# Token statistics of six of sixteen batches on ScalarE, and new step lists for the opening

## The chip, the cores and the metric

The kernel runs on one core of a Trainium2 chip. The metric is the device time of one execution in microseconds (us). The kernel before takes 1945.47 us, the median of three runs (1943.98 to 1945.88).

## What is computed

The input `x` is 16 batches of 512 tokens of 256 numbers, f32. Each token is normalised, and the result goes two ways: through an attention layer with a feed-forward block, and through a gated network whose operands are rounded to a 4-bit grid in blocks of 16. Cut to what matters here:

```
xn = (x - mean(x)) / sqrt(var(x) + 1e-5)          # per token; also needed summed over the tokens of a batch
pooled = xn.mean(axis=1)                           # one row of 256 per batch, all 16 batches
gl  = pooled @ gate_w + gate_b + einsum(pooled @ mod_w + mod_b, mod_basis)
wts = topk_sparse(gl)                              # 16 heads x 16 modes per batch
kern_masks = einsum(amps, sin(freqs . position + phases))
kern = einsum(wts, kern_masks)                     # 16 heads x 512 lags per batch
scores = 3 * step(kern) * window + q bias + k bias + 0.15 * qc . kc / sqrt(8)
s = LN(h + ffn(h)),  h = LN(xn + softmax(scores) @ v @ out_w + out_b)
g = silu(fp4_linear(silu(fp4_linear(xn, w_gate)) * fp4_linear(xn, w_up), w_down))
out = x + s * g
```

The kernel masks need `pooled` of all sixteen batches, so before any batch's scores can be finished, the statistics (mean and variance of each token) of all of `x` must have been taken.

## The kernel before

Tokens lie on the 128 partitions, four tiles `t` to a batch (`[128, 4, 256]`). The program has three parts: a head (steps named `pre:`, `pro:` and `first:`), a loop over batches 1 to 14 (`mid`), and an end. On each of the five engines the steps of a part stand in an order written out by hand in the table `ORDER`; an engine does its steps strictly in that order, and waits at a step's semaphores with everything behind it. The change touches the head's five lists, and the steps `st` and `cp`; the loop and the end are as they were.

In the head, `pre:` is the work that is common to all batches, `pro:` the first half of batch 0, `first:` the rest of batch 0 together with the start of batch 1.

- `px.n` (SyncE) loads batch n into one of NX = 4 buffers (`hY`, `y2`, shown as `y` in the trace, `xnb`, `catT`). From n = 4 on it waits until TensorE's sum of batch n - 4 has let go of the buffer.
- `st.n` (VectorE) takes the statistics: four BN_STATS, a small copy, four BN_AGGR, and the addition of eps into `p_ve`. `rs.n` (GpSimd) raises that to the power -1/2. `cp.n` (VectorE) files mean and 1/std with three small copies, the last into `v_cur`, from which TensorE reads its weights.
- `sum.n+1` (TensorE) adds batch n, weighted by 1/std, to the sums in PSUM (8 passes); `sum.0` clears the sums, `sum.17` takes the means off. `pre:pooled` (VectorE) reads them.
- `arg.h`, `rnd.h`, `fr.h`, `sin.h` for 16 heads: TensorE makes the arguments, ScalarE rounds them, VectorE takes the fraction, ScalarE the sine. `arg.h` waits for `fr.h-4`, since there are four PSUM banks.
- `pre:ones` (GpSimd) is three large memsets, of `KS`, `QS` and `v_new`.
- `pro:norm`, `xT`, `proj.0` to `.2`, `projm`, `splitio`, `load.0`, `load.1`: batch 0 is normalised, transposed, projected, split into bf16 parts, and goes to DRAM and back. `pro:v.0` and `.1` make the values, `mx.h.p.u` are the tiles of the row maxima (TensorE computes 20 of them for half 0, VectorE reduces each).
- `ws.i` (VectorE), `wm.i` (GpSimd), `wr.i` (VectorE), `wt` (TensorE, ScalarE): the three matrices of the gated network are rounded and transposed.
- After `pre:pooled`: `modT`, `peak`, `topk`, `kw`, `soft` (VectorE) with `mod`, `gl`, `wide`, `kern` (TensorE) and the first loads `first:T` of the kernel's rows.

Of the kernel before, what the change touches and what calls it, by code (L numbers as in the profile page):

```python
# [56 lines left out]
class Event:  # L57
# [5 lines left out]
    def wait(self, eng, b, k=None):  # L63

        if isinstance(b, int) and b < 0:
# [10 lines left out]
            pre:px.0 pre:waves pre:px.1 pre:px.2 pre:ld.w_proj pre:px.3 pro:xload pre:px.4 pre:px.5 pre:px.6 pre:px.7  # L76
            pre:ld.w_gate pre:ld.w_v pre:ld.basis pre:ld.c0 pre:px.8 pre:ld.c1 pre:ones pre:px.9 pro:splitio pre:px.10
            pre:px.11 pro:load.0 pre:px.12 pre:px.13 pre:px.14 pre:px.15 pro:load.1 pre:ld.c2 pre:ld.w_rest pre:rz
            first:xload pro:mio.0 pre:rows first:T.0 first:T.1 first:splitio first:T.2 first:T.3 first:mio.1 first:T.4
            first:load.0 first:T.5 first:T.6 first:T.7 first:mio.0  # L80
        """,
        gpsimd="""
            pre:iota pre:half pre:rs.0 pre:rs.1 pre:rs.2 pre:rs.3 pre:rs.4 pre:rs.5 pre:rs.6 pre:ones pro:projm.0
            pre:rs.7 pro:projm.1 pro:projm.2 pre:wm.0.0 pre:rs.8 pre:rs.9 pre:rs.10 pre:rs.11 pre:wm.0.1 pre:wm.1.0
            pre:rs.12 pre:rs.13 pre:rs.14 pre:rs.15 pre:wm.1.1 pro:xq first:xnb pre:wm.2.0 pre:wm.2.1 pro:xr first:xq
            first:projm.0 first:xr first:projm.1 first:projm.2 first:mul.0 first:mul.1 first:mul.2 first:hq.0
            first:mul.3 first:hr.0 first:hq.1 first:mul.4 first:hq.2 first:mul.5 first:hr.1 first:hr.2 first:mul.6
            first:mul.7 first:hq.3 first:hr.3
        """,
        vector="""  # L90
            pre:zero pre:st.0 pre:cp.0 pre:st.1 pre:cp.1 pre:st.2 pre:fr.0 pre:fr.1 pre:cp.2 pre:st.3 pre:fr.2
            pre:cp.3 pre:fr.3 pro:norm pre:st.4 pre:fr.4 pre:st.5 pre:fr.5 pre:st.6 pre:cp.4 pre:st.7 pro:proj.0
            pre:fr.6 pre:fr.7 pre:fr.8 pre:cp.5 pre:cp.6 pre:fr.9 pro:xq pro:proj.1 pre:fr.10 pro:proj.2 pre:ws.0
            pre:fr.11 pre:st.8 pre:fr.12 pre:fr.13 pre:cp.7 pre:wr.0 pre:st.9 pre:ws.1 pre:cp.8 pre:cp.9 pro:v.0
            pro:v.1 pre:st.10 pre:st.11 pre:fr.14 pre:cp.10 pro:mx.0.0.0 pro:mx.0.0.1 pro:mx.0.0.2 pro:mx.0.0.3
            pro:mx.0.0.4 pro:mx.0.1.0 pro:mx.0.1.1 pro:mx.0.1.2 pro:mx.0.1.3 pro:mx.0.1.4 pro:mx.0.2.0 pro:mx.0.2.1
            pro:mx.0.2.2 pro:mx.0.2.3 pro:mx.0.2.4 pro:mx.0.3.0 pro:mx.0.3.1 pre:cp.11 pre:st.12 pre:st.13 pre:st.14
            pre:cp.12 pre:st.15 pre:cp.13 pro:mx.0.3.2 pro:mx.0.3.3 pro:mx.0.3.4 pre:cp.14 pre:cp.15 pro:mfin.0 pre:mr
            pre:wr.1 pre:pooled pre:fr.15 pre:poolT first:mx.1.0.0 pre:modT pre:peak first:mx.1.0.1 pre:topk pro:xr
            pre:kw pre:ws.2 first:mx.1.0.2 first:mx.1.0.3 first:norm pro:xr2 pre:wr.2 first:mx.1.0.4 first:mx.1.1.0  # L100
            first:mx.1.1.1 first:mx.1.1.2 pre:soft first:proj.0 first:xq first:proj.1 first:xr first:v.0 first:proj.2
            first:xr2 first:mx.1.1.3 first:mx.1.1.4 first:muld.0.0 first:mx.1.2.0 first:mx.1.2.1 first:mx.1.2.2
            first:muld.0.1 first:mx.1.2.3 first:muld.1.0 first:muld.1.1 first:mx.1.2.4 first:mx.1.3.0 first:mx.1.3.1
            first:mx.1.3.2 first:mx.1.3.3 first:mx.1.3.4 first:mfin.1 first:muld.2.0 first:silu.0.0 first:muld.2.1
            first:silu.0.1 first:muld.3.0 pre:pad first:hq.0 first:muld.3.1 first:v.1 first:hr.0 first:silu.1.0
            first:silu.1.1 first:muld.4.0 first:hq.1 first:muld.4.1 first:silu.2.0 first:mx.0.0.0 first:silu.2.1
            first:muld.5.0 first:mx.0.0.1 first:mx.0.0.2 first:hq.2 first:mx.0.0.3 first:muld.5.1 first:hr.1
            first:mx.0.0.4 first:mx.0.1.0 first:dn.0 first:ctxt.0 first:muld.6.0 first:silu.3.0 first:mx.0.1.1
            first:mx.0.1.2 first:silu.3.1 first:hr.2 first:muld.6.1 first:mx.0.1.3 first:mx.0.1.4 first:mx.0.2.0
            first:muld.7.0 first:mx.0.2.1 first:ctxt.1 first:muld.7.1 first:mx.0.2.2 first:mx.0.2.3 first:mx.0.2.4  # L110
# [1579 lines left out]
```

## Time and the profile before

| | us |
|---|---|
| median of 3 runs | 1945.47 |
| the profiled execution | 1947.52 |
| its span, first to last instruction | 1945.7 |
| first tile of the row maxima on VectorE | from 75.93 |
| `pre:pooled` on VectorE | from 115.56 |
| `pre:soft` on VectorE | from 153.79 |
| end of the head (`cT`, the first step of the loop on TensorE) | from 252.64 |

The profiled execution lies 1.8 us over its span, and 2.05 us over the median. In the rows below a time is us from the span's start. PE is TensorE, PEld its weight loads, DVE VectorE, ACT ScalarE, POOL GpSimd, SP SyncE.

### The profile page before, as it was taken

The page shows a single profiled execution, that of the slowest core. Times are in us where ns is not written, and L with a number is a line of the kernel's source. Part 1 is how long each engine was busy: PE and PEld are TensorE (multiplying, and loading weights), DVE is VectorE, ACT ScalarE, POOL GpSimd, SP SyncE. Part 2 cuts the span into 40 slices and gives each one's busy share as a digit, 9 for nine tenths or more (in the row PEclk, how much of TensorE's full clock was granted, in tenths as well). Part 3 has the DMA queues.
Part 4 walks back from the last instruction along what each step waited for, and adds up shares of the span by engine and source line. Part 5 has one row for each costly group of instructions (what it writes and reads, how often), then busy time and mean ns, then how long its engine had stood idle before and what let it go on. Part 6 is the DMA issues. An engine that isn't in the chain of part 4 may idle for free.

```text
span 1945.7 us, 42571 instructions
## 1 busy us (share of the span) xinstructions
PE 1820.7 (94%) x12700; PEld 1311.4 (67%) x12700; DVE 1615.3 (83%) x5197; ACT 901.9 (46%) x1833; POOL 1103.7 (57%) x799
## 2 busy tenths in 40 slices
PE   8667999999999999999999999999999999999997
PEld 3234677676776767677776767677676767677766
DVE  7868879888898988888997988888897988889763
ACT  3024454454635445453545445463545445363542
POOL 3434746565664746465674756466574656566563
PEclk8777999999999999999999999999999999999999
DMA  5343223232223333232322323222332323322211
GB/s 170 117 123 89 64 74 108 65 105 73 77 74 83 108 73 95 65 103 70 93 76 73 107 75 95 73 82 71 99 90 73 107 62 103 77 78 74 63 56 33
DMA packets 138566, 165.35 MB, mean 85 GB/s; under 512 B 19758, under 2 KB 100655, under 8 KB 138453
## 3 DMA queue, kind: packets, MB, share of 16 engines
q1 hardware_dynamic: 138458, 164.30, 30.5%
q14 instruction: 87, 0.70, 0.1%
q8 instruction: 21, 0.34, 0.1%
HBM read 127.85 MB, written 36.41 MB: 84 GB/s over the span
## 4 chain that ended last, share of the span: by engine, by line
PE 60%; DVE 15%; issue 12%; POOL 6%; ACT 3%; DMA 3%; SPq 1%; DVEq 0%; ACTq 0%; POOLq 0%
PE ps L767 11%; PE ps L758 11%; PE ps L699 8%; PE ps L716 4%; PE ps L622 3%; PE ps L609 3%; PE ps L656 3%; PE ps L595 3%; POOL Pr L1174 3%; PE ps L672 2%; PE ps L731 2%; PE ps L652 2%; DVE st L956 2%; DVE nmax L1035 2%; DMA QS<-q_bias_parts 2%
## 5 line engine op out<-in xcount | busy, mean ns | idle before, releaser
L1174 POOL TENSOR_TENSOR Pr<-Pr,Tz 128x768 f32<-128x768 f32 (+2 forms) x384 | 478.2, 1275 | 248.5 <-ACT Pr L831 244.6
L1035 DVE CUSTOM_DVE_ANT_0 ps<-ps,future 128x512 f32<-128x512 f32 (+3 forms) x1024 | 474.6, 516 | 51.2 <-issue 50.9
L831 ACT ACTIVATE Pr<-ps 128x384 f32<-128x384 f32 x512 | 243.8, 489 | 352.7 <-PE ps L656 348.6
L622 PE MATMUL ps<-KS,QS 108*128 108x512 bf16 (+3 forms) x1024 | 218.3, 304 | 32.5 <-DVE nmax L1035 23.9
L758 PE MATMUL ps<-catT,w 128*128 128x256 f32 x1024 | 237.8, 380 | 0.7 <-ACT catT L894 0.7
L767 PE MATMUL ps<-w,gT 128*128 128x256 f32 x1024 | 232.9, 381 | 0.9 <-ACT gT L911 0.9
L1065 DVE SCALAR_TENSOR_TENSOR Pr<-ps,Tz 128x512 f32<-128x512 f32 x256 | 175.2, 684 | 54.7 <-ACT ps L820 46.7
L820 ACT ACTIVATE ps<-ps 128x512 f32<-128x512 f32 x256 | 150.4, 588 | 139.9 <-PE ps L652 138.4
L767 PEld LDWEIGHTS ps<-w,gT 128*128 128x128 f32 x1024 | 190.8, 190 | 25.7 <-ACT gT L911 1.3
L758 PEld LDWEIGHTS ps<-catT,w 128*128 128x128 f32 x1024 | 189.6, 190 | 26.3 <-ACT catT L894 0.9
L716 PE MATMUL ps<-wdT,hqT 128*128 128x256 f32 x768 | 178.0, 381 | 0.7 <-ACT hqT L870 0.7
L656 PE MATMUL ps<-QS,KS 112*128 112x384 bf16 (+2 forms) x768 | 162.7, 276 | 16.1 <-DVE Pr L1065 11.7
L699 PE MATMUL ps<-wgT,xqT 128*128 128x352 f32 x512 | 176.0, 466 | 0.2 <-ACT xqT L851 0.2
L699 PE MATMUL ps<-wuT,xqT 128*128 128x352 f32 x512 | 172.4, 459 | 0.0
L1213 POOL TENSOR_TENSOR slot<-slot 128x704 f32<-128x704 f32 x64 | 107.6, 1681 | 97.5 <-DVE slot L939 97.5
L622 PEld LDWEIGHTS ps<-KS,QS 108*128 108x128 bf16 x1024 | 88.2, 98 | 106.7 <-DVE nmax L1035 48.5
L1223 POOL TENSOR_TENSOR rstd<-ve,minus_half 128x4 f32<-128x4 f32 (+1 forms) x34 | 33.4, 982 | 223.4 <-DVE ve L964 222.0
L716 PEld LDWEIGHTS ps<-wdT,hqT 128*128 128x128 f32 x768 | 142.4, 190 | 20.1 <-ACT hqT L870 1.1
L672 PE MATMUL ps<-Pr,v_cur 128*17 128x128 f32 (+2 forms) x3584 | 152.5, 321 | 0.6 <-ACT hqT L870 0.6
L1035 DVE DVE_READ_ACCUMULATOR2_ANT nmax<- 128x1 f32 x1024 | 142.7, 139 | 0.0
L699 PEld LDWEIGHTS ps<-wuT,xqT 128*128 128x128 f32 x512 | 97.2, 190 | 54.4 <-ACT ctxT L846 0.3
L672 PEld LDWEIGHTS ps<-Pr,v_cur 128*17 128x17 f32 x3584 | 95.2, 98 | 53.2 <-issue 40.8
(226 smaller groups left out, 3252.0 us busy)
## 6 DMA issues: line engine op xcount, KB each, us to landing
Tz<-kernel_rows SPq DMA_DIRECT2D x256, 256.0 KB, 3.5
KS<-k_parts SPq DMA_DIRECT2D x32, 384.0 KB
QS<-q_parts SPq DMA_DIRECT2D x64, 192.0 KB
hY<-in_x SPq DMA_DIRECT2D x19, 512.0 KB, 4.8
xn<-in_x SPq DMA_DIRECT2D x17, 512.0 KB, 3.5
out<-y SPq DMA_DIRECT2D x15, 512.0 KB, 3.0
q_parts<-q_sp SPq DMA_DIRECT2D x16, 384.0 KB, 3.1
k_parts<-k_sp SPq DMA_DIRECT2D x16, 384.0 KB, 2.4
```

Source lines behind the costliest of these rows:

```text
L622: ins = mm(o, QS[0:KROWS, 2 * p + e, it * P:(it + 1) * P], KS[0:KROWS, p, 0:n], start=True, stop=True)
L656: ins = mm(dst[:, at:at + PAST[j]], KS[0:SROWS, p, j * P:(j + 1) * P], rhs[:, S - 1:P * (j + 1) - 1:-1], start=True, stop=True)
L672: ins = mm(dst[32 * hh:32 * hh + HD + 1, to:to + n], v_cur[:, j, 4 * g + hh, :], rhs[:, n - 1::-1], start=i == 0, stop=i == len(pieces) - 1)
L699: ins = mm(dst[:, 0:IH], xqT[:, c, t * P:(t + 1) * P], wt[:, c, f * IH:(f + 1) * IH], start=c == 0, stop=c == KD - 1)
L716: ins = mm(dst[:, 0:D], hqT[:, c * P:(c + 1) * P], wdT[:, c, :], start=c == 0, stop=c == KI - 1)
L758: ins = mm(dst[:, i * n:(i + 1) * n], w1[:, c, f * P:(f + 1) * P], catT[:, c, hf * n:(hf + 1) * n], start=c == 0, stop=c == KD - 1)
L767: ins = mm(dst[:, 0:D], gT[:, f, at:at + P], w2[:, f, :], start=f == 0, stop=f == KF - 1)
L820: inc(af(src, src, ACT.Exp), "a_exp")
L831: inc(af(Pr[:, p % 4, e, at:at + wd], src[:, 0:wd], ACT.Exp), "a_exp")
L1035: ins = v.tensor_tensor_reduce(o, o, future[:, S - n:S], -1.0, 3e38, ALU.add, ALU.min, nmax[:, 2 * pl + e, it:it + 1])
L1065: v.scalar_tensor_tensor(blocks(Pr[:, p % 4, e, 0:S]), blocks(ps[:, SC_BANKS[n % len(SC_BANKS)], :]), 3e38, near, ALU.min, ALU.mult).then_ ...
L1174: ins = g.tensor_tensor(a, a, Tz[:, p % 2, :, P * j:P * j + PAST[j]], ALU.mult)
```

## The change

The statistics of batches 5, 7, 9, 11, 13 and 15 are taken by ScalarE, in two passes over the data: a Copy of each of the four tiles with an accumulated output gives the sum, one small Copy turns the four sums into minus the mean, and a Square of each tile with that as bias and an accumulated output gives the sum of squared differences. VectorE's `st.n` of these batches is then one small instruction (divide by 256, add eps) that waits for ScalarE (`rowsq`), and the first of the copies in `cp.n` becomes a division by 256. A new buffer `junk` takes the outputs that nobody reads. The counts of the semaphore `stats` follow the ten batches that are left.

```diff
+        ACT_STATS = [5, 7, 9, 11, 13, 15]
+        junk = sb("junk", [P, T, D])
...
+                if n in ACT_STATS:
+                    dve.wait_ge(L["rowsq"], ACT_STATS.index(n) + 1)
+                    v.tensor_scalar(p_ve[:, i, :], p_st[:, i, :, 2], 1.0 / D, EPS, ALU.mult, ALU.add).then_inc(L["var"], 1)
+                    return
+                k2 = 2 * sum(m not in ACT_STATS for m in range(n))
                 for t in range(T):
                     ins = v.bn_stats(p_st[:, i, t, :], x_in[i][:, t, :])
                 ins.then_inc(L["stats"], 1)
-                dve.wait_ge(L["stats"], 2 * n + 1)
+                dve.wait_ge(L["stats"], k2 + 1)
...
+                if n in ACT_STATS:
+                    v.tensor_scalar(mean_all[:, T * n:T * (n + 1)], p_st[:, i, :, 0], 1.0 / D, None, ALU.mult)
+                else:
+                    v.tensor_copy(mean_all[:, T * n:T * (n + 1)], p_mv[:, i, :, 0])
...
+            elif k == "st":
+                n = s[1]
+                i, m = n % NX, ACT_STATS.index(n)
+                act.wait_ge(x_sem[i], 16 * (n // NX + 1))
+                if n >= NX:
+                    act.wait_ge(L["mean"], n - NX + 1)
+                if m:
+                    act.wait_ge(L["rowsq"], m)
+                for t in range(T):
+                    ins = af(junk[:, t, :], x_in[i][:, t, :], ACT.Copy, accum_out=p_st[:, i, t, 0:1])
+                ins.then_inc(L["rowsum"], 1)
+                act.wait_ge(L["rowsum"], 2 * m + 1)
+                af(p_st[:, i, :, 1], p_st[:, i, :, 0], ACT.Copy, scale=-1.0 / D).then_inc(L["rowsum"], 1)
+                act.wait_ge(L["rowsum"], 2 * m + 2)
+                for t in range(T):
+                    ins = af(junk[:, t, :], x_in[i][:, t, :], ACT.Square, bias=p_st[:, i, t, 1:2], accum_out=p_st[:, i, t, 2:3])
+                ins.then_inc(L["rowsq"], 1)
```

All five lists of the head are laid out anew. The diff of them is a table of names; what it does is shown here at three places, as the instructions then stand in an engine's stream. In SyncE's list `px.2` to `px.7` stand behind more of the weight loads, and the first load of batch 1 behind `mio.0`; on TensorE eleven `arg` steps and the transposes of batch 0 now come ahead of the first sum, and `sum.9` ahead of `pro:v.0`; the remaining rows of the lists are permutations of the same steps.

First, GpSimd at its first statistics step. Before (KS, QS and v_new are the memsets of `pre:ones`, p_rstd is `rs.n`):

```order
L1357 MEMSET minus_half 128x4
L1373 TENSOR_TENSOR p_rstd<-p_ve,minus_half 128x4 x7
L1353 MEMSET KS 128x4096
L1354 MEMSET QS 128x4096
L1355 MEMSET v_new 128x1088
L1166 TENSOR_TENSOR q_sp<-q_r,q_sp 128x512
```

And with the change:

```order
L1358 MEMSET minus_half 128x4
L1374 TENSOR_TENSOR p_rstd<-p_ve,minus_half 128x4
L1354 MEMSET KS 128x4096
L1355 MEMSET QS 128x4096
L1356 MEMSET v_new 128x1088
L1374 TENSOR_TENSOR p_rstd<-p_ve,minus_half 128x4 x4
```

The three memsets stood behind the seventh `rs`, and stand now behind the first.

Second, VectorE from its first statistics on. Before (L1414 to L1422 are `st`, L1429 to L1431 `cp`, all of batch 0 and then batch 1):

```order
L1414 BN_STATS p_st<-hY 128x6 x4
L1417 COPY p_ve<-p_st 128x4
L1419 BN_AGGR p_mv<-p_st 128x2 x4
L1422 TENSOR_SCALAR p_ve<-p_mv 128x4
L1429 COPY mean_all<-p_mv 128x4
L1430 COPY rstd_all<-p_rstd 128x4
L1431 COPY v_cur<-p_rstd 128x4
L1414 BN_STATS p_st<-y 128x6 x4
```

With the change (L1444 is `fr`, L992 `pro:norm`, L1420 the next `st`):

```order
L1444 SCALAR_TENSOR_TENSOR Pr<-Pr,ps 128x512
L1438 COPY mean_all<-p_mv 128x4
L1439 COPY rstd_all<-p_rstd 128x4
L1440 COPY v_cur<-p_rstd 128x4
L1444 SCALAR_TENSOR_TENSOR Pr<-Pr,ps 128x512 x6
L992 TENSOR_SCALAR xn<-xn,mean_all,rstd_all 128x256 x4
L1420 BN_STATS p_st<-y 128x6 x4
```

One `fr` comes ahead of the copies of batch 0, six more and the normalisation of batch 0 come directly behind them, and the statistics of batch 1 after all of that.

Third, ScalarE at its first new step, and VectorE where that is waited for. ScalarE with the change (L1613 is `rnd`, L1617 `sin`, L1627 to L1633 the statistics, first of batch 5 and then of batch 7):

```order
L1613 ACTIVATE Pr<-ps,round_c 128x512 x2
L1627 ACTIVATE junk,p_st<-y 128x256 x4
L1630 ACTIVATE p_st<-p_st 128x4
L1633 ACTIVATE junk,p_st<-y,p_st 128x256 x4
L1613 ACTIVATE Pr<-ps,round_c 128x512
L1617 ACTIVATE Pr<-Pr 128x512
L1627 ACTIVATE junk,p_st<-catT 128x256 x4
```

VectorE there (L1460 is the last instruction of `ws.0`, L1416 the short `st.5`, then `st.6`, and L1436 of the short `cp.5`):

```order
L1460 TENSOR_SCALAR gs_old<-gs_old 128x96
L1416 TENSOR_SCALAR p_ve<-p_st 128x4
L1420 BN_STATS p_st<-xnb 128x6 x4
L1423 COPY p_ve<-p_st 128x4
L1425 BN_AGGR p_mv<-p_st 128x2 x4
L1428 TENSOR_SCALAR p_ve<-p_mv 128x4
L1436 TENSOR_SCALAR mean_all<-p_st 128x4
```

No table load of ScalarE stands between these steps and the sines around them. VectorE's short step stands at the place of a whole `st`, and everything behind it waits with it for ScalarE.

## Rows read from the trace of the kernel before

**Rows 1.** The page: span, and each engine's busy time.

```profile
span 1945.7 us, 42571 instructions
PE 1820.7 (94%) x12700; PEld 1311.4 (67%) x12700; DVE 1615.3 (83%) x5197; ACT 901.9 (46%) x1833; POOL 1103.7 (57%) x799
```

**Rows 2.** Windows: PE, PEld, DVE, ACT, POOL busy (xinstructions), then clock, DMA share, GB/s.

```profile
0.00:115.56 115.56, 84.46 (x255) 32.77 (x255) 91.01 (x357) 24.33 (x40) 43.19 (x40) 0.79 0.57 167
75.93:115.56 39.63, 29.71 (x108) 10.24 (x108) 28.35 (x151) 4.20 (x7) 16.28 (x11) 0.82 0.60 174
115.56:153.79 38.23, 19.59 (x95) 11.48 (x95) 29.13 (x85) 7.49 (x9) 13.52 (x7) 0.70 0.06 18
176.56:252.64 76.08, 68.15 (x538) 44.20 (x539) 61.88 (x207) 34.07 (x74) 49.91 (x39) 0.89 0.26 79
```

**Rows 3.** The timeline at the head's checkpoints, and one row of three `fr`.

```profile
7.93 0.69 ACT L1604 ACTIVATE Pr<-ps,round_c 128x512 f32<-128x512 f32 x1 [2.82 <-PE ps L1543]
...
8.07 0.17 DVE L1429 COPY mean_all<-p_mv 128x4 f32<-128x4 f32 x1 [1.28 <-POOL p_rstd L1373]
...
39.49 1.87 DVE L1435 SCALAR_TENSOR_TENSOR Pr<-Pr,ps 128x512 f32<-128x512 f32 x3
...
49.13 0.35 DVE L1008 SCALAR_TENSOR_TENSOR bias_r<-ps,bb,bias_sp 128x128 f32<-128x128 f32 x1 [2.23 <-ACT bias_sp L798]
...
75.93 0.69 DVE L1035 CUSTOM_DVE_ANT_0 ps<-ps,future 128x512 f32<-128x512 f32 x1
...
115.56 0.41 DVE L1463 TENSOR_SCALAR ctxn<-ps 16x256 f32<-16x256 f32 x1 [2.86 <-PE ps L1535]
...
153.79 1.73 DVE L1504 TENSOR_SCALAR Tz<-Pr 128x2048 f32<-128x2048 f32 x1
```

**Rows 4.** The timeline around 31 us, GpSimd and VectorE.

```profile
30.82 3.51 POOL L1353 MEMSET KS<- 128x4096 bf16 x1
31.34 7.41 DVE L1417 COPY p_ve<-p_st 128x4 f32<-128x4 f32 x1
...
34.27 3.51 POOL L1354 MEMSET QS<- 128x4096 f32 x1
...
37.72 1.00 POOL L1355 MEMSET v_new<- 128x1088 f32 x1
```

**Rows 5.** The timeline, one batch's statistics on VectorE.

```profile
27.70 1.40 DVE L1414 BATCH_NORM_STATS2 p_st<-xnb 128x6 f32<-128x256 f32 x4
...
29.61 0.17 DVE L1422 TENSOR_SCALAR p_ve<-p_mv 128x4 f32<-128x4 f32 x1
29.69 0.16 DVE L1429 COPY mean_all<-p_mv 128x4 f32<-128x4 f32 x1
```

**Rows 6.** The timeline, ScalarE: eight instructions in a row with a bias, eight without.

```profile
278.30 3.16 ACT L911 ACTIVATE gT<-ps,b 128x256 f32<-128x256 f32 x8
...
153.91 1.58 ACT L1622 ACTIVATE wgT<-ps 128x128 f32<-128x128 f32 x8 [9.21 <-PE ps L1589]
```

**Rows 7.** The page's groups: an accumulator read on VectorE.

```profile
L1035 DVE DVE_READ_ACCUMULATOR2_ANT nmax<- 128x1 f32 x1024 | 142.7, 139 | 0.0
```

**Rows 8.** The timeline, TensorE: a sum at either clock, and a projection at the low one.

```profile
17.75 3.59 PE L1530 MATMUL ps<-y,v_cur 128*16 128x256 f32 x8
...
45.16 1.90 PE L1530 MATMUL ps<-y,v_cur 128*16 128x256 f32 x8
...
30.64 3.78 PE L595 MATMUL ps<-xnT,cq 128*128 128x512 f32 x4
```

**Rows 9.** Two stretches of 2 us: busy times, then clock.

```profile
18.00:20.00 2.00, 2.00 (x6) 0.74 (x5) 1.65 (x7) 0.55 (x1) 0.32 (x1) 0.50 0.00 0
46.00:48.00 2.00, 2.00 (x8) 0.81 (x7) 0.91 (x2) 0.17 (x1) 0.00 (x0) 1.00 1.07 353
```

**Rows 10.** The chain that ended last, 90 to 116 us: start, length, what.

```profile
96.29 6.80 DMA catT<-in_x
...
113.72 1.74 PE ps L1535 x8
```

More of the change, by code:

```diff
@@ L75 @@
         sync="""
[L76 to L80, printed above, removed]
+            pre:px.0 pre:waves pre:px.1 pre:ld.w_proj pro:xload pre:px.2 pre:px.3 pre:ld.w_gate pre:px.4 pre:ld.w_v
@@ L81 @@
+            pre:ld.basis pre:ld.c0 pre:px.5 pre:px.6 pre:ones pre:ld.c1 pre:px.7 pre:px.8 pre:px.9 pro:splitio
+            pre:px.10 pro:load.0 pre:px.11 pre:px.12 pre:px.13 pre:px.14 pre:px.15 pro:load.1 pre:ld.c2 pre:ld.w_rest
+            pro:mio.0 pre:rz first:xload pre:rows first:T.0 first:T.1 first:splitio first:T.2 first:T.3 first:mio.1
+            first:T.4 first:load.0 first:T.5 first:T.6 first:T.7 first:mio.0
         """,
         gpsimd="""
-            pre:iota pre:half pre:rs.0 pre:rs.1 pre:rs.2 pre:rs.3 pre:rs.4 pre:rs.5 pre:rs.6 pre:ones pro:projm.0
@@ L84 @@
[L84 to L88, printed above, removed]
+            pre:iota pre:half pre:rs.0 pre:ones pre:rs.1 pre:rs.2 pre:rs.3 pre:rs.4 pro:projm.0 pro:projm.1
@@ L89 @@
         """,
         vector="""
[L91 to L110, printed above, removed]
@@ new lines @@
+            pre:mr pro:mfin.0 pre:wr.1 pre:pooled pre:fr.15 pre:poolT first:mx.1.0.0 pre:modT pre:peak first:mx.1.0.1
+            first:mx.1.0.2 pre:topk pre:kw pre:ws.2 first:mx.1.0.3 pro:xr first:norm pro:xr2 pre:wr.2 first:mx.1.0.4
+            first:mx.1.1.0 first:mx.1.1.1 first:mx.1.1.2 pre:soft first:proj.0 first:xq first:proj.1 first:proj.2
+            first:mx.1.1.3 first:mx.1.1.4 first:mx.1.2.0 first:mx.1.2.1 first:xr first:xr2 first:muld.0.0 first:v.0
+            first:muld.0.1 first:mx.1.2.2 first:mx.1.2.3 first:muld.1.0 first:mx.1.2.4 first:mx.1.3.0 first:mx.1.3.1
@@ new lines @@
+            pre:sum.13 pre:sum.14 pro:mx.0.3.4 pre:sum.15 pre:sum.16 pre:sum.17 first:mx.1.0.0 pre:poolT pre:mod
+            pre:gl first:mx.1.0.1 first:mx.1.0.2 first:mx.1.0.3 pro:mT.0 pre:wt.0 pre:wide pre:kern pre:wt.1
+            first:mx.1.0.4 first:mx.1.1.0 first:mx.1.1.1 pre:wt.2 pre:wt.3 first:mx.1.1.2 first:xT.0 first:xT.1
+            first:proj.0 pre:wt.4 pre:wt.5 pre:wt.6 pre:wt.7 pre:wt.8 first:proj.1 first:proj.2 first:sc.0.0 pro:xqT
+            first:sc.0.1 first:mx.1.1.3 first:mx.1.1.4 first:mx.1.2.0 pre:join first:mx.1.2.1 first:gu.0.0
```

109 lines of the change are left out of this document (61 added, 48 removed).

## Prediction

> **What bounds the kernel now.** The page comes first: TensorE is busy 94% of the span and VectorE 83% [rows 1], but these are means over a long loop that the change doesn't touch. So I cut the head out by windows. Up to `pre:pooled` (115.56 us) VectorE is busy 91.0 us, TensorE 84.5 and ScalarE 24.3 [rows 2]; TensorE's clock is 0.79 of full speed there, so it isn't at its peak. From 115.56 to 153.79 VectorE has 29.1 of 38.2 us; in the last 76 us TensorE leads with 68.2 [rows 2]. The order is fixed on each engine, and everything behind `pooled` (gates, masks, `soft`, first scores) waits for it. So the question is how early `pooled` and then `soft` come [rows 3]; behind them the same work stands as before, and I carry a shift there one for one to the end.
>
> VectorE's 91.0 us aren't all work. At 31.34 a copy of `[128, 4]` takes 7.41 us instead of 0.17, and its row ends at 38.75, where GpSimd's three memsets end (30.82 to 38.72) [rows 4]. So 7.2 us of the busy time are a blocked copy; useful work is 83.8 us, and idle 115.6 - 91.0 = 24.6 us.
>
> **The change part by part.**
>
> *Work taken from VectorE.* One batch's statistics last from 27.70 to 29.69, where the next step's copy begins: 1.99 us [rows 5]. Six times is 11.9 us. Each leaves one small instruction (0.08 from start to start, 29.61 to 29.69 [rows 5]), 0.5 us in all. Useful work up to `pooled` falls by 11.4 us, from 83.8 to 72.4. No other VectorE step crosses `pooled`, by the two lists.
>
> *Work given to ScalarE.* The trace has no Copy or Square with an accumulated output. From below: eight instructions of 256 columns with a bias take 3.16 us, 0.395 each; 128 columns without one 0.20 each [rows 6]. A batch is 4 Squares at 0.395, 4 Copies at some 0.30 (between these two rows) and one small Copy at 0.2: 3.0 us, if accumulating is free. From above: a second instruction as long as the short one, 0.20, for each of the eight gives 4.6. VectorE's own accumulator read is 0.14 [rows 7], and being the same kind of operation it is what I take: 3.0 + 8 x 0.14 = 4.1, and with two waits on its own results 4.3 us a batch. Six are 26 us, on an engine that idles 91 of 115.6 us [rows 2]: hidden, except where VectorE's short step meets an unfinished ScalarE.
>
> *The blocked copy.* The memsets stand now behind `rs.0`, so they run from about 8.0 (in the rows `cp.0` starts at 8.07, as soon as `rs.0` is done [rows 3]) to 15.9, 7.9 us later. VectorE does one `fr` first: its rounding ends at 8.6 [rows 3] and it takes 0.6 (three in 1.87 [rows 3]), so the three copies of `cp.0` are due at 9.2 and get through at 15.9. The stall isn't removed but moved: 6.7 us in place of 7.2. The Trainium skill has a rule for this (SBUF — State Buffer, "Who interferes with whom"): VectorE and GpSimd share a port pair that one holds for a whole instruction, and copies in the two-port mode ask for it. The trace agrees with its 7.41 us. It speaks against the new place, since there too plain copies meet the memsets; without the rule one might expect no stall, and the sum below would be 6.7 us smaller.
>
> What is behind the copies: six `fr`, `norm`, and the whole statistics of batches 1 to 3; on TensorE `arg.5` on, since `arg.h` waits for `fr.h-4`.
>
> *The new front.* TensorE now has eleven `arg` before the first sum. Half speed is the level of 1.2 GHz: at clock 0.50 a sum takes 3.59 us, at 1.00 1.90; the four passes of a projection take 3.78 at the low one, so some 1.9 at the full [rows 8, 9]. An `arg` is two passes of that width, half of 3.78, and 1.7 in a row, where one begins before the last has ended. The engine stands idle before 16.8, so I take `arg.5` to `arg.10` low: 10.3 us, to 27.1. The transposes and `sum.0` take 2, `sum.1` 3.5 (low): 32.6. Then `proj.0`, `sum.2`, `proj.1`, `sum.3` at full clock, 1.9 each, and `proj.2` 0.8: 41. VectorE's last projection step, at 49.13 before [rows 3], comes about 41.2. But by then VectorE lacks work that it had done before (`fr.7` to `.10` at 0.6, `cp.3` to `.6` at 0.22, `st.6` at 2.0: 5.3 us). At equal work the change is ahead by 2.6 us only. In this stretch VectorE runs dry: it has done `xq` by 30.6 and has 3.2 us of work till 41.2, so 7.4 us idle.
>
> *New waits.* (1) `st.5` stands at the head of VectorE's queue behind `ws.0`; ScalarE begins it when batch 5 has landed, near 45, and ends near 49.3, some 1.5 us late. (2) `st.7` stands behind `rnd.13` on ScalarE, that waits for `arg.13`, that for `sum.7`, that for `cp.6`: some 2 us late. (3) `wr.0` waits for GpSimd's product and `ws.0` for its load: 3.5 together. Then `v.0` and `v.1` wait on TensorE for `sum.8` and `sum.9`: two sums and the values at mixed clock, 3.5 us of waiting. From the first maximum tile to `pooled` the rows have 39.6 us with 28.4 busy [rows 2]. The same steps stand there now, but `st.13` and `st.15` are short: 28.4 - 2 x 1.9 = 24.6 us of work. The idle 11.3 us came from sums of batches 8 to 10 between the tiles, from the load of batch 15 (6.8 us) and from the last sums, each 1.7 us [rows 10]. Now TensorE has two of these sums ahead of the values, and batch 15 can be loaded some 10 us behind the first tile instead of 20; I take 4.1 us of waits, an estimate of mine, for `sum.10` to `sum.12` between the tiles and for the last one. That makes 28.7 us.
>
> *The ledger up to `pooled`.* Useful 72.4, blocked 6.7, idle 4.0 (start, till 9.2) + 7.4 + 7.0 (waits 1 to 3) + 3.5 + 4.1 = 26.0. Sum 105.1 us, against 115.6: 10.5 earlier. The first maximum tile comes at 105.1 - 28.7 = 76.4, so no earlier than 75.93 [rows 3]; the gain shows behind it, because the sums are further on and their batches wait less.
>
> *Behind `pooled`.* The same VectorE steps. One more maximum tile stands before `topk` (0.8 later), and the 1.4 us of `pro:xr`, which filled VectorE's wait for `wide`, stands behind it now: I take 1 us lost in the 38.2. Table loads: by the lists there are two fewer of ScalarE, at a place where it waits anyway: nothing. From `soft` on, VectorE's order to the first score changes, but the load of the kernel's rows sets it: nothing, with 3 us either way for the 76 us of the new `first` list.
>
> Sum: 10.5 - 1.0 = 9.5 us. The profiled execution 1947.5 - 9.5 = 1938.0; the median lies 2.05 below that execution: 1936 us.
>
> **The rivals.**
>
> *The gain is larger: the waits don't come.* If TensorE is at full clock for the `arg` steps and sums (as for part of 12 to 15 us), the front is shorter by up to 6 x 0.85 = 5 us, and waits 1 to 3 shrink too. All 7 us of those two give 1929. For it: DMA and ScalarE have room. Against: clock 0.79 in the head [rows 2]. Chance 0.25.
>
> *The gain goes into the front.* `sum.1` comes at 32 instead of 9 us, so batch 4 is loaded 20 us later than now, and if every TensorE step from 27 on runs at the low clock, `proj.2` comes 6 us later (four steps at 3.6 instead of 1.9). Then 9.5 - 6 to 7 leaves about 3: 1943, and a little more makes it no change. For it: the low clock right after `arg` steps (0.50 at 18 to 20 us [rows 9]). Against: under a steady load the clock came back in that stretch each time. Chance 0.17.
>
> *Slower: ScalarE's statistics are what VectorE waits for.* VectorE meets them at its queue's head at `st.5`, `st.7`, `st.9` and, through `cp.15`, at `pooled`. Each us over 4.3 for a batch is paid up to four times; 9.5 / 4 = 2.4, so from 6.7 us a batch the gain is gone, and from 7.7 the kernel is 4 us slower, 1949.5. That would be 0.9 us for an instruction whose nearest row is 0.395 [rows 6]. Such a price could come from table loads, but the lists have none there. Chance 0.06.
>
> *The change does what it says to VectorE, but `first` gives it back.* The last 76 us are TensorE's (68.2 busy [rows 2]) and newly ordered; 5 us lost there leave 4.5: 1941. This lies in the main range. The forecast itself has 0.52.
>
> **How the numbers follow.** Main range: ScalarE's price from 3.0 to 4.6 moves two to four waits by up to 1.3 us down and 0.3 up, 3 up and 1 down in all; `first` gives 3 either way, the clock in the front 3: 1931 to 1941. To hold 8 in 10 I reach to 1929 below and 1943 above. 0.2% (3.9 us) is about what a measurement of this kernel can tell from no change: up to 1941.6 is faster. Faster: 0.52 + 0.25 + a quarter of the front case, 0.04 = 0.81. Same: the rest of that case, 0.12, and 0.01. Slower: the ScalarE case, 0.06.
>
> **What would show it.** Right: a copy of `cp.0` of 6 to 7 us beside the memsets at 8 to 16; no such row at 31; `bias_r` near 41; the first maximum tile near 76; `pooled` near 105 and `soft` near 144; the loop's first `cT` some 9 us before 252.6. ScalarE's statistics take 4 us a batch, with a row of its own for the accumulator. Wrong in a step: `pooled` on time but `cT` not earlier (`first`); waits of VectorE for ScalarE of 3 us and more at the short steps (its price); no blocked copy at 9 us. What would make the forecast wrong as a whole is most likely what is late between 41 and 76 us, where one wait replaces another and I have placed four of them by estimate.

## The result, and the profile after

The changed kernel takes 2046.03 us (median of 4 runs, 2044.12 to 2050.88) against 1945.68 of the kernel before on the same chip: ratio 1.0521, 95% interval 1.0500 to 1.0542. It is 5% slower, and the forecast was 1936.

The page of the kernel after, which answers to [rows 1], and one row of its DMA queues:

```profile
span 2045.5 us, 42628 instructions
PE 1860.2 (91%) x12700; PEld 1332.3 (65%) x12700; DVE 1641.4 (80%) x5143; ACT 925.3 (45%) x1933; POOL 1110.6 (54%) x799
...
q14 instruction: 99, 0.81, 0.1%
```

TensorE has 40 us more of busy time for the same 12,700 matmuls, and queue 14, which brings instructions, has 99 packets; in the kernel before it was 87. VectorE has 54 instructions fewer, and 26 us more of busy time.

First the opening, in windows as in [rows 2] (up to `pooled`, the first maximum tile to `pooled`, `pooled` to `soft`, the last 76 us ahead of the loop):

```profile
0.00:113.23 113.23, 82.74 (x251) 31.94 (x251) 80.15 (x302) 49.28 (x144) 40.45 (x38) 0.85 0.57 170
81.78:113.23 31.45, 24.61 (x96) 8.63 (x96) 24.46 (x132) 13.76 (x48) 7.81 (x6) 0.84 0.67 202
113.23:155.57 42.34, 24.32 (x113) 14.67 (x113) 29.28 (x85) 6.05 (x13) 17.76 (x9) 0.61 0.06 17
174.46:250.54 76.08, 68.80 (x555) 45.68 (x555) 65.64 (x203) 33.44 (x74) 51.18 (x38) 0.96 0.31 91
```

The timeline of VectorE at the checkpoints of [rows 3], with the copies that meet GpSimd's memsets (here 7.84 to 15.75, [rows 4] before) and the two short steps that wait for ScalarE:

```profile
9.43 6.34 DVE L1438 COPY mean_all<-p_mv 128x4 f32<-128x4 f32 x1
...
40.26 0.35 DVE L1007 SCALAR_TENSOR_TENSOR bias_r<-ps,bb,bias_sp 128x128 f32<-128x128 f32 x1 [1.40 <-ACT bias_sp L797]
...
49.85 0.17 DVE L1416 TENSOR_SCALAR p_ve<-p_st 128x4 f32<-128x4 f32 x1 [2.25 <-ACT junk L1633]
...
53.40 2.57 DVE L1438 COPY mean_all<-p_mv 128x4 f32<-128x4 f32 x1
...
65.37 1.54 DVE L1416 TENSOR_SCALAR p_ve<-p_st 128x4 f32<-128x4 f32 x1 [4.30 <-ACT junk L1633]
...
79.47 0.75 DVE L1018 TENSOR_TENSOR v_new<-ps,row_v_b 128x256 f32<-128x256 f32 x2 [3.57 <-PE ps L608]
...
81.78 0.69 DVE L1034 CUSTOM_DVE_ANT_0 ps<-ps,future 128x512 f32<-128x512 f32 x1
...
113.23 0.41 DVE L1472 TENSOR_SCALAR ctxn<-ps 16x256 f32<-16x256 f32 x1
...
155.57 3.25 DVE L1513 TENSOR_SCALAR Tz<-Pr 128x2048 f32<-128x2048 f32 x1
```

So the opening isn't where 100 us went: `pooled` comes 2.3 us earlier than before, `soft` 1.8 later, the loop's first `cT` at 250.54, 2.1 earlier. The loss is in the loop, whose steps the change doesn't touch. A window from the loop's first `cT` to its fifteenth (14 iterations), in before and in after, with two single iterations of after between them, the first and the fourth:

```profile
252.64:1801.13 1548.49, 1502.51 (x10865) 1111.71 (x10864) 1329.27 (x4270) 761.27 (x1540) 915.99 (x658) 1.00 0.31 84
```

```profile
250.54:361.10 110.56, 107.32 (x777) 79.33 (x776) 94.75 (x305) 54.36 (x110) 65.41 (x47) 1.00 0.31 85
598.00:717.49 119.49, 111.76 (x778) 82.05 (x777) 97.74 (x305) 54.62 (x110) 65.89 (x47) 0.96 0.28 78
250.54:1900.97 1650.43, 1543.32 (x10865) 1132.46 (x10864) 1363.79 (x4270) 764.45 (x1540) 922.15 (x658) 0.97 0.28 79
```

Same counts of instructions, 101.9 us more. And the first iteration is as fast as before (110.56 us); every later one takes 117 to 120. Whatever is wrong, then, isn't in what the loop's instructions do but in coming round to them again.

The same place in two iterations, from the timelines of VectorE, GpSimd and TensorE. Before (the iteration's `cT` is at 473.73):

```profile
477.70 0.69 DVE L1133 TENSOR_TENSOR hY<-ps,xnb 128x512 f32<-128x512 f32 x1 [2.94 <-PE ps L731]
479.43 0.69 DVE L1133 TENSOR_TENSOR hY<-ps,xnb 128x512 f32<-128x512 f32 x1 [1.03 <-PE ps L731]
...
487.63 1.67 DVE L978 SCALAR_TENSOR_TENSOR hY<-hY,rstd,row_ln_b 128x256 f32<-128x256 f32 x4
...
489.22 3.73 POOL L1174 TENSOR_TENSOR Pr<-Pr,Tz 128x768 f32<-128x768 f32 x3 [6.00 <-ACT Pr L831]
```

After (`cT` at 478.28):

```profile
482.34 0.69 DVE L1132 TENSOR_TENSOR hY<-ps,xnb 128x512 f32<-128x512 f32 x1 [3.02 <-PE ps L730]
486.97 0.69 DVE L1132 TENSOR_TENSOR hY<-ps,xnb 128x512 f32<-128x512 f32 x1 [3.94 <-issue]
...
495.17 4.22 DVE L977 SCALAR_TENSOR_TENSOR hY<-hY,rstd,row_ln_b 128x256 f32<-128x256 f32 x4
...
495.79 4.19 POOL L1173 TENSOR_TENSOR Pr<-Pr,Tz 128x768 f32<-128x768 f32 x3 [5.02 <-ACT Pr L830]
...
499.52 1.96 PE L747 MATMUL ps<-ident,hY 128*128 128x128 f32 x8 [3.54 <-DVE hY L977]
...
504.48 3.62 PE L757 MATMUL ps<-catT,w 128*128 128x256 f32 x8
```

Three things happen one after the other. (1) Between the two sums into `hY` VectorE stands for 3.94 us, and the reason is "issue": it waited for nothing that the profile shows. Before, it waited there 1.03 us for TensorE, so it is 2.9 us late. (2) Its group L977 starts 16.9 us behind `cT` instead of 13.9. Before, the group was over (489.30) just when GpSimd's products began (489.22); now the products begin 0.6 us into it, the two run into each other, and the group takes 4.22 us instead of 1.67, another 2.55. (3) TensorE waits 3.54 us for it, and behind the wait its clock is at the lower level, as three windows of the kernel after show:

```profile
496.00:499.50 3.50, 0.00 (x0) 0.00 (x0) 3.50 (x5) 0.58 (x1) 3.50 (x3) 0.84 0.00 0
499.50:504.00 4.50, 4.12 (x20) 3.12 (x21) 3.57 (x16) 2.76 (x6) 4.50 (x3) 0.50 0.38 117
504.00:508.20 4.20, 4.20 (x11) 2.98 (x10) 2.07 (x10) 0.63 (x2) 0.60 (x1) 0.50 0.37 125
```

0.50 is 1.2 GHz; eight matmuls of L757 take 3.62 us there, and 1.89 a little later. The iteration is 9.2 us longer than before; 2.9 and 2.55 are named, and the remaining 3.7 fit 8.7 us of TensorE at half speed, which is 4.35 us of work lost. Not every iteration loses as much. The 13 slow ones are 7.8 us longer in the mean, and they differ with the clock: the second takes 117.18 us at a granted clock of 0.99, the ninth 118.64 at 0.97, the fourth 119.49 at 0.96.

The packets of queue 14 bear this out, though the profile doesn't say which engine one of them is for. In the iteration above the kernel after has one that starts between 480.0 and 480.4 us (480.14), and the next between 484.6 and 485.0 (484.76, landed at 485.26):

```profile
q14 instruction: 1, 0.01, 7.1%
```

```profile
q14 instruction: 1, 0.01, 7.8%
```

The second sum starts at 486.97. In all 13 iterations from the second on the second packet starts 4.4 to 5.0 us behind the first, and the second sum 1.6 to 1.8 us behind the second packet's landing. In before the same two packets come behind each jump (475.60 and 479.99 in the iteration shown), and the second sum, at 479.43, doesn't wait for the second of them. In the first iteration there is no such pair in either kernel.

### The profile page after: what moved, and what is told of

It is laid out like the page before. It is cut to its first block, busy times and chain, and to the rows that moved or that the text cites. A ratio compares the mean times of both kernels' runs of the same rounds, so it can differ in the third digit from the quotient of the medians.

```text
span 2045.5 us, 42628 instructions
## 1 busy us (share of the span) xinstructions
PE 1860.2 (91%) x12700; PEld 1332.3 (65%) x12700; DVE 1641.4 (80%) x5143; ACT 925.3 (45%) x1933; POOL 1110.6 (54%) x799
## 4 chain that ended last, share of the span: by engine, by line
PE 59%; DVE 17%; issue 15%; POOL 5%; ACT 3%; DVEq 1%; ACTq 0%; DMA 0%; POOLq 0%; SPq 0%
PE ps L757 11%; PE ps L766 10%; PE ps L698 8%; PE ps L715 4%; PE ps L621 3%; PE ps L655 3%; PE ps L730 3%; POOL Pr L1173 3%; PE ps L608 3%; PE ps L594 3%; PE ps L651 2%; PE ps L671 2%; DVE hY L977 2%; DVE st L955 2%; DVE nmax L1034 1%
## 5 line engine op out<-in xcount | busy, mean ns | idle before, releaser
L1173 POOL TENSOR_TENSOR Pr<-Pr,Tz 128x768 f32<-128x768 f32 (+2 forms) x384 | 485.0, 1292 | 297.6 <-ACT Pr L830 294.3
L621 PE MATMUL ps<-KS,QS 108*128 108x512 bf16 (+3 forms) x1024 | 227.2, 315 | 29.9 <-DVE nmax L1034 27.5
L757 PE MATMUL ps<-catT,w 128*128 128x256 f32 x1024 | 248.2, 392 | 0.7 <-ACT catT L893 0.7
L757 PEld LDWEIGHTS ps<-catT,w 128*128 128x128 f32 x1024 | 197.8, 198 | 30.1 <-DVE slot L1104 2.7
L1064 DVE SCALAR_TENSOR_TENSOR Pr<-ps,Tz 128x512 f32<-128x512 f32 x256 | 175.2, 684 | 48.2 <-ACT ps L819 41.2
L655 PE MATMUL ps<-QS,KS 112*128 112x384 bf16 (+2 forms) x768 | 168.5, 285 | 32.1 <-DVE Pr L1064 28.8
L655 PEld LDWEIGHTS ps<-QS,KS 112*128 112x128 bf16 x768 | 68.8, 101 | 101.6 <-DVE Pr L1064 56.4
```

What stands on the lines that cost most here:

```text
L621: ins = mm(o, QS[0:KROWS, 2 * p + e, it * P:(it + 1) * P], KS[0:KROWS, p, 0:n], start=True, stop=True)
L655: ins = mm(dst[:, at:at + PAST[j]], KS[0:SROWS, p, j * P:(j + 1) * P], rhs[:, S - 1:P * (j + 1) - 1:-1], start=True, stop=True)
L757: ins = mm(dst[:, i * n:(i + 1) * n], w1[:, c, f * P:(f + 1) * P], catT[:, c, hf * n:(hf + 1) * n], start=c == 0, stop=c == KD - 1)
L1064: v.scalar_tensor_tensor(blocks(Pr[:, p % 4, e, 0:S]), blocks(ps[:, SC_BANKS[n % len(SC_BANKS)], :]), 3e38, near, ALU.min, ALU.mult).then_ ...
L1173: ins = g.tensor_tensor(a, a, Tz[:, p % 2, :, P * j:P * j + PAST[j]], ALU.mult)
```

## The experiments

Theory A: it is the place of the code, as just told. Theory B: the loop has settled into a slower pattern because of the order in which the opening leaves the engines. Theory C: it is ScalarE's statistics, their buffer or their semaphores. D against E is about the second half: a collision that follows from the delay, or more missing instructions. F, G, H, I are about the opening, J and K about the border. Fillers are memsets of one element each, to a buffer of their own that nothing reads; nothing else of the computation is changed in them. Numbers of single runs are compared with before on the same chip, 1947 to 1948 us.

**a_v8: 8 fillers ahead of `st.5`.** 

```diff
+                for _ in range({5: 8}.get(n, 0)):
+                    v.memset(filler[:, used[0]:used[0] + 1], 0.0)
+                    used[0] += 1
                 dve.wait_ge(x_sem[i], 16 * (n // NX + 1))
```

> The kernel after, with 8 one-element memsets more in VectorE's opening, where it waits 2.25 us for ScalarE's fifth statistics. In the compiled stream VectorE's loop body moves from instructions 707 to 1170 to 715 to 1178. Expected: an iteration from the second on takes 110.6 us in place of 117 to 120, the packets of queue 14 fall from 99 to about 87, and the time is 1942 to 1946 us. Theory B (the opening hands the engines over in an order in which the loop settles into a slower pattern): 8 short instructions inside a wait change nothing, 2046 us. Theory C (the statistics on ScalarE, their buffer or their two semaphores slow the loop): 2046 us too.

**a_v3: 3 fillers** at the same place.

> The same with 3 memsets in place of 8: the loop body at 710 to 1173, still two instructions ahead of the border at 712. Theory A: as slow as the kernel after, iterations of 117 to 120 us, 2040 to 2050 us, the stall now at the 3rd loop instruction. Theories B and C: 2046 us. If it is as fast as the kernel with 8, the border is not where theory A puts it, or any small shift in time cures the loop.

**a_s8: 8 fillers on ScalarE**, an Identity of one element each, behind `rnd.15`.

> The kernel after, with 8 one-element ACTIVATEs more on ScalarE in the opening (behind its 16th rounding) and VectorE's code as it is. Theory A: VectorE's loop lies where it lay, so 2046 us, iterations of 117 to 120 us. A theory by which ScalarE's code, which moved by 106 instructions, is what stalls, or by which any small shift helps, expects another time: near 1945 us.

**b_v79: the kernel before with 79 fillers**, 13 ahead of `st.4` and 6 ahead of each from `st.5` to `st.15`.

> The kernel before, statistics all on VectorE and its own lists, with 79 one-element memsets more spread over VectorE's opening. Its loop body moves from 757 to 1220 to 835 to 1298, which is the place of the kernel after plus 128. Theory A: the loop of before becomes as slow as that of after, iterations of 117 to 120 us and the same 3-us stall at the 6th loop instruction, 2030 to 2055 us with up to 5 us for the memsets. Theories B and C: iterations of 110.6 us, 1946 to 1951 us.

Measured: a_v8 1947.59 us, ratio to before 0.9992 (0.9983 to 1.0002); a_v3 2050.03; a_s8 2037.12; b_v79 2050.97. The windows over the same 14 iterations, in this order:

```profile
251.92:1801.72 1549.80, 1502.90 (x10865) 1112.51 (x10864) 1329.02 (x4270) 761.28 (x1540) 915.54 (x658) 1.00 0.31 84
```

```profile
252.38:1902.81 1650.43, 1539.88 (x10866) 1130.78 (x10865) 1356.77 (x4270) 764.11 (x1540) 920.90 (x658) 0.97 0.29 79
```

```profile
251.10:1890.77 1639.67, 1537.16 (x10866) 1128.58 (x10864) 1357.49 (x4270) 763.82 (x1540) 920.78 (x658) 0.98 0.29 80
```

```profile
249.83:1904.50 1654.67, 1545.60 (x10866) 1133.65 (x10865) 1362.71 (x4270) 763.99 (x1540) 921.48 (x658) 0.97 0.29 79
```

Eight instructions that compute nothing take 100 us off. Three don't, and they move the stall as theory A says. The timeline of VectorE in a_v3, and in b_v79 for the kernel before:

```profile
609.22 1.29 DVE L1132 TENSOR_TENSOR hY<-ps,xnb 128x512 f32<-128x512 f32 x2 [8.50 <-issue]
```

```profile
606.11 0.69 DVE L1133 TENSOR_TENSOR hY<-ps,xnb 128x512 f32<-128x512 f32 x1 [4.30 <-issue]
```

With 3 fillers the border has come ahead of the first of the two `hY` sums, and the wait stands there; both then run in a row. In b_v79 nothing of the change is in the kernel, and it is as slow as after, with the stall between the two sums again. So A holds, and B and C fall: the statistics on ScalarE had nothing to do with the 100 us. a_s8 came out 9 us below what A expected. Its slow iterations were 114.5 to 120.5 us. In the two shortest (114.5 and 114.8) the second sum comes 5.6 and 5.9 us behind the first, later than in any other, against 4.7 in the iteration from 478.63, and the group L977 then runs just ahead of GpSimd's products, four times 0.48 us with no collision; the others differ with the clock (0.96 to 0.99), as in after. Why the second packet comes sooner in one iteration than in another stays open.

**a_swap: GpSimd's first product behind `lnb1`**, otherwise the kernel after.

```diff
-            ln1 mul.0 lnb1 xnb mul.1
+            ln1 lnb1 mul.0 xnb mul.1
```

> The kernel after with its code where it was (body 707 to 1170), and one change in GpSimd's loop list: the product mul.0 behind lnb1 in place of ahead of it. In the kernel after VectorE's four hY operations of L977 run into GpSimd's three products of L1173: two take 2.02 and 1.48 us in place of 0.48 each, the group 4.21 in place of 1.67. Theory D (the 3-us stall makes VectorE late, so that it meets GpSimd's products, and this collision is the other half of the loss): without the product there the group takes 1.67 us again and an iteration 112.5 to 115.5 us, the time 1975 to 2010 us, with the first stall still there. Theory E (the later stalls are instruction stalls of their own): the group still takes some 4.2 us and an iteration 117 to 120 us, 2046 us.

**b_hold: before, with VectorE held by work.** Its two reductions write to a buffer that nothing reads.

```diff
                 elif k == "out":
                     u = s[1]
+                    if which == "mid" and u == 1:
+                        for i, m in enumerate((w1, w2)):
+                            v.tensor_reduce(hold[:, i:i + 1], m[:].rearrange("p k n -> p (k n)"), AX.X, ALU.max)
```

> The kernel before with two VectorE reductions of 128x2048 added in the loop ahead of the step out.1, each some 2.3 us (a reduction of 128x704 took 0.81), so that out.1 comes 3.3 to 3.6 us later than in before, about as late as in after, but by work and not by missing instructions; the loop's code keeps its place (757 to 1222). Theory D: the loop loses as much as in the kernel after, iterations of 116 to 120 us, with hY rows of 1.5 to 2 us beside GpSimd's products: 2030 to 2060 us. Theory E: only the delay itself counts, at most 3.6 us an iteration, 110.6 to 114.2 us, 1946 to 1996 us.

Measured: a_swap 1995.98 us, b_hold 2069.34. The 14 iterations of a_swap, and its group of L977 in the timeline of VectorE:

```profile
250.54:1849.49 1598.95, 1520.93 (x10866) 1115.23 (x10864) 1329.28 (x4270) 764.76 (x1540) 915.54 (x658) 0.99 0.30 82
```

```profile
485.19 0.69 DVE L1132 TENSOR_TENSOR hY<-ps,xnb 128x512 f32<-128x512 f32 x1 [5.15 <-issue]
...
493.40 1.67 DVE L977 SCALAR_TENSOR_TENSOR hY<-hY,rstd,row_ln_b 128x256 f32<-128x256 f32 x4
```

And b_hold, its 14 iterations and the same place:

```profile
255.13:1922.93 1667.80, 1556.10 (x10865) 1139.65 (x10864) 1425.84 (x4298) 764.16 (x1540) 922.22 (x658) 0.96 0.28 78
```

```profile
496.87 4.47 DVE L1132 TENSOR_REDUCE hold<-w 128x1 f32<-128x2048 f32 x2
...
509.44 4.22 DVE L979 SCALAR_TENSOR_TENSOR hY<-hY,rstd,row_ln_b 128x256 f32<-128x256 f32 x4
```

D holds. In a_swap the stall is there (5.15 us in this iteration), the collision isn't, and half of the loss is gone: 114.2 us an iteration, the clock back at 0.99. What the same swap does to the kernel before was not run; b_hold makes the argument without it. In b_hold no instruction is missing, VectorE is simply 3.3 us late (the second `hY` sum starts 5.0 us behind the first, before 1.7), and the group takes 4.22 us, the iteration 119.5, the same as in after; here the first iteration is slow too (117.2), since nothing depends on the jump. The whole kernel is 9 us over my range, of which 7 are its first iteration and 2.5 an opening that ended later.

**b_v10: before with 10 fillers**, one ahead of each of `st.4` to `st.13`.

> The kernel before with 10 one-element memsets more in VectorE's opening. 
Measured 1946.46 us. Its 14 iterations, and from its page the row of queue 14:

```profile
249.28:1799.93 1550.65, 1502.78 (x10866) 1110.53 (x10865) 1332.77 (x4270) 761.42 (x1540) 915.42 (x658) 1.00 0.31 84
```

```profile
q14 instruction: 99, 0.81, 0.1%
```

J holds: this kernel fetches as many packets as after, 99 (a_v8: 86), and its iterations take 110.76 us, within 0.2 of before. Its compiled stream has the body one place earlier than the text above says, at 766 to 1229, so that 74 instructions lie ahead of the border; the argument is the same. Not the number of packets counts, but whether one is wanted right behind the jump.

**a_none and a_late4: the new lists with no statistics, or with four, on ScalarE.**

```diff
-        ACT_STATS = [5, 7, 9, 11, 13, 15]
+        ACT_STATS = [9, 11, 13, 15]
```

This is a_late4; in a_none the list is empty. The steps that are no longer in it go from ScalarE's list as well.

> All five lists of after, but all sixteen statistics on VectorE as before. VectorE's loop body lies at 756 to 1219 with no filler, so the loop should run at 110.6 us. It separates the new order from ScalarE's statistics. By the prediction's ledger (statistics worth 11.4 us of VectorE, less the waits for ScalarE of 2.3 and 4.3 us) it should be some 4 to 9 us slower than the kernel after with the loop put right (1947.6 against 1948.4 for before): 1951 to 1957 us. Rival: in the opening VectorE isn't what is waited for, and what it gets off its hands only turns into waits: 1946 to 1949 us.

> The lists of after, with the statistics of batches 5 and 7, for which VectorE waited 2.25 and 4.30 us, back on VectorE (2.0 us each), those of 9, 11, 13 and 15 on ScalarE. The loop body lies at 724 to 1187, so the loop runs at 110.6 us. Theory F (these two waits are where the opening's gain went): the first maximum tile comes 2 to 4 us earlier than in after (81.8), the time is 1943 to 1946 us. Rival G (the sums on TensorE and the loads set the pace, the waits stand beside them): no change against the kernel after with 8 memsets, 0.999 of before.

**b_late4 and b_late3: the old lists** with `pre:st.9` behind `rnd.13`, `st.11` behind `rnd.14`, `st.13` and `st.15` behind `rnd.15` on ScalarE; b_late3 without `st.9`. **a_late4_again** is a_late4 unchanged.

> The five lists of before, with the statistics of batches 9, 11, 13 and 15 on ScalarE (between its roundings 13 to 15) and the rest of the change's code. VectorE's loop body lies at 724 to 1187, clear of the border. The new lists cost something by themselves: with all statistics on VectorE they gave 1.0016 of before, with these four on ScalarE 0.9988, so moving the four is worth 0.28%, 5.5 us. Theory H (both add up): with the old lists it gives 0.9972 of before, 1941 to 1944 us, with pooled at 108 to 112 us in place of 115.6. Rival I (in the old lists the loads and TensorE's sums set the pace from 76 to 115 us, the chain had 6.80 us of a load): 0.998 to 1.000.

> The same with the statistics of batches 11, 13 and 15 on ScalarE, batch 9's on VectorE, where it precedes the values. Theory H: 0.998, a quarter less gain than with four. Rival I: no change, 0.999 to 1.000.

> The kernel with the lists of after and four statistics on ScalarE once more, beside the two with the old lists. Expected again 0.9976 to 1.000 of before, and slower than the old lists with the same four by theory H, the same by rival I.

All have their loop clear of the border and run it at 110.6 us. Checkpoints from each timeline, and the ratio to before from the timed runs (the row of before has the checkpoints of [rows 3] and its median beside a_none and a_late4; beside the last three of the experiments it was 1947.33, beside a_v8 1948.37). The checkpoints are of one execution, the medians of 11 or 12; the execution shown for b_late4 is the slowest of its 12 (1950.19), that of b_late3 the fastest (1942.35):

| kernel | lists | on ScalarE | first tile | `pooled` | `soft` | loop's first `cT` | median us | ratio (95%) |
|---|---|---|---|---|---|---|---|---|
| before | old | 0 | 75.93 | 115.56 | 153.79 | 252.6 | 1948.0 | 1 |
| b_late3 | old | 3 | 71.66 | 109.12 | 147.43 | 247.7 | 1948.33 | 1.0002 (0.9988 to 1.0016) |
| b_late4 | old | 4 | 78.09 | 115.84 | 155.15 | 254.3 | 1945.89 | 0.9994 (0.9984 to 1.0004) |
| a_none | new | 0 | 81.32 | 117.33 | 159.68 | 254.7 | 1951.70 | 1.0016 (1.0003 to 1.0029) |
| a_late4 | new | 4 | 81.79 | 113.39 | 155.72 | 250.5 | 1945.69 | 0.9988 (0.9976 to 1.0000) |
| a_late4_again | new | 4 | 82.26 | 114.80 | 157.12 | 252.1 | 1945.79 | 0.9990 (0.9980 to 0.9999) |
| a_v8 | new | 6 | 83.05 | 114.73 | 157.07 | 251.9 | 1947.59 | 0.9992 (0.9983 to 1.0002) |

a_none lies in the range expected for it (1951 to 1957), and its rival falls. Within the new lists the four statistics are worth 0.28% (0.9988 against 1.0016), 5.5 us, and the lists by themselves cost 0.16%, at the edge of what a measurement can tell. The 5.5 us in the text for b_late4 is taken from these two kernels and was no forecast. H falls: the old lists with the same four give nothing that can be told from before. More I can't say of the old lists, because their opening scatters (the loop begins at 247.7 to 254.3 us in these, and at 252.6, 249.8 and 249.3 in three kernels with the opening of before, fillers apart). a_late4, the only one of them measured twice, lies below before in both measurements, by 0.1%, which is less than the 0.2% that I took for the least a measurement can tell.

F was wrong in its mechanism, though the time lies in its range (G had named 0.999 as well). Without the two waits for ScalarE the first tile comes at 81.79, in after at 81.78. The timeline of VectorE in a_late4, where it does the statistics of batch 7 itself:

```profile
62.16 1.62 DVE L1423 COPY p_ve<-p_st 128x4 f32<-128x4 f32 x1
...
64.09 2.57 DVE L1428 TENSOR_SCALAR p_ve<-p_mv 128x4 f32<-128x4 f32 x1
...
79.48 0.76 DVE L1018 TENSOR_TENSOR v_new<-ps,row_v_b 128x256 f32<-128x256 f32 x2 [3.83 <-PE ps L608]
```

Two instructions of 0.17 us take 1.62 and 2.57, and 64.09 + 2.57 = 66.66 is where GpSimd's product of the gate weights ends (63.83 to 66.63 in its timeline). In after VectorE waits 4.30 us for ScalarE in the same stretch, and its short step, too, is held (1.54 us at 65.37, to 66.91) until GpSimd is done. So the second wait for ScalarE was the cover of another. The first, 2.25 us, was worth no more than the 2.0 us that VectorE now spends on batch 5's statistics itself: GpSimd's three products, which wait for VectorE, begin at 60.17 in a_late4 and at 60.43 in after. From 72 us on both wait for two of TensorE's sums and the values.

## Why the prediction was wrong

- **"... behind them the same work stands as before, and I carry a shift there one for one to the end."** This is the step that failed, and with 101.9 us it decides the case. I read the loop as untouched because none of its lines is. But a loop's code has a place too, and the head's instruction count sets it. The diff shows that VectorE's opening gets shorter, and a page with a DMA queue for instructions (87 packets in before) says that they are fetched while the kernel runs; I put the two together nowhere. My rivals were all about the opening, and none of them ends near 2046; the one on the slower side gave 1949.5.
- **Work taken from VectorE, and the blocked copy: right.** Useful work and blocked copy should have come to 72.4 + 6.7 = 79.1 us up to `pooled`; VectorE is busy 80.15. The copies of `cp.0` took 6.34 us from 9.43 on, where 6.7 from 9.2 was forecast. What I hadn't seen is the next collision, `cp.6` at 53.40 with 2.57 us.
- **Work given to ScalarE: right.** A batch takes 4.0 us, forecast 4.3. Its timeline, one of four from either pass:

```profile
45.67 0.42 ACT L1627 ACTIVATE junk<-y 128x256 f32<-128x256 f32 x1
45.98 0.20 ACT L1627 ACTIVATION_READ_ACCUMULATOR junk<-y 128x1 f32 x1
...
47.65 0.51 ACT L1633 ACTIVATE junk<-y,p_st 128x256 f32<-128x256 f32 x1
48.06 0.19 ACT L1633 ACTIVATION_READ_ACCUMULATOR junk<-y,p_st 128x1 f32 x1
```

  The accumulator has a read of its own, 0.20 where I took 0.14, but half of it lies beside the next instruction: 0.40 from one to the next in the first pass.
- **The new front: right.** `bias_r` came at 40.26, forecast 41.2; VectorE idled 9.6 us from 9.43 to 40.26, not 7.4. The six `arg` took 10.60 us, forecast 10.3 at the low clock, and ended at 26.5, forecast 27.1:

```profile
15.88 10.60 PE L1552 MATMUL ps<-ctxT,Tz 6*128 6x512 f32 x12 [0.99 <-DVE Pr L1444]
26.41 1.97 PE L584 MATMUL ps<-ident,xn 128*128 128x128 f32 x8
```

  The windows give a clock of 1.00 here, but the profile of this execution has no entry for the clock before 30.8 us, and 1.00 is what a window then shows. The durations tell more: eight transposes of this form take 1.96 us at a clock of 0.50 (499.52, above) and 1.04 at 1.00 (478.28), and here 1.97. So TensorE was at 1.2 GHz, as I had taken it to be, and the condition of my rival with the larger gain didn't come about. The 0.85 of the first window is too high for the same reason.
- **New waits: too small.** VectorE's idle time up to `pooled` is 113.23 - 80.15 = 33.1 us; I had 26.0. The waits for ScalarE are 2.25 and 4.30 (forecast 1.5 and 2), and from the first tile to `pooled` it idles 31.45 - 24.46 = 7.0 instead of 4.1, though its work there is the 24.6 that I had. So `pooled` came at 113.2, not 105.1. As a_late4 shows, the time to the first tile isn't won back by giving these two batches back to VectorE: for the first it works as long as it had waited, and behind the second wait stands GpSimd.
- **Behind `pooled`: 4.1 us lost, forecast 1.** 42.34 us to `soft`, against 38.2 in [rows 2], with TensorE's clock at 0.61 in place of 0.70. The one more tile and `pro:xr` that I had priced at 1 us aren't enough; which instructions make up the rest I only read in a_late4, with the same 42.3 us: a wait for TensorE's `gl` 1.1 us longer (its matmuls run at the low clock there), an instruction of 0.69 us that takes 2.67 beside GpSimd, and 1.3 us ahead of the last tile.
- **`first` gives nothing either way: wrong in size.** The 98.9 us from `soft` to the loop became 95.0, 3.9 us won.
- The opening as a whole: 2.1 us of the forecast 9.5. With the loop put right (a_v8) the change is worth 0.1%, not told from nothing. "The gain goes into the front" was the rival that came nearest to that: 1943, "and a little more makes it no change". That is luck: the front came on time, and what was lost was lost behind it.
